# Regrouping the waits ahead of the last stores of a graph layer with a routed feed-forward part

## What is computed

```python
logits = xf @ router_w.T + router_b
idx = jnp.argmax(logits, axis=-1)
h = relu(einsum('nd,ndh->nh', xf, W1[idx]) + b1[idx])      # 256 -> 64
out = relu(einsum('nh,nhd->nd', h, W2[idx]) + b2[idx])     # 64 -> 256
x = x + out
```

## Time and profile before

| | us |
|---|---|
| median of 3 runs | 648.89 |
| lowest and highest | 646.72 and 649.28 |
| the profiled execution's own time | 648.73 |
| its span | 647.0 |
| POOL's last gather ends (in the span) | 591.7 |
| first of the 25 stores starts | 599.86 |
| last addition on DVE ends | 636.77 |
| last store starts | 640.76 |

### The profile page before, as it was taken

The page is one execution under the profiler, slowest core; times in us unless marked ns, Lnnn a source line. Parts: engine busy times, 40 slices in busy tenths (PEclk is TensorE's granted clock), DMA queues, the critical chain, the costliest instruction groups (busy, mean ns, idle before and its releaser), DMA issues.

```text
span 647.0 us, 10654 instructions
## 1 busy us (share of the span) xinstructions
PE 543.5 (84%) x3190; PEld 444.8 (69%) x3191; DVE 399.5 (62%) x1372; ACT 200.9 (31%) x406; POOL 443.4 (69%) x465
## 2 busy tenths in 40 slices
PE   0777998998888866899999999998999993289990
PEld 0676997866666665686878787886878762167880
DVE  6868776533343345455776767677566776716883
ACT  4666700000000010215552424242242452045540
POOL 6777777777777777777777777777777700374555
PEclk9969999999999987999999999999999996579996
DMA  8983333333333444334444544454444418464112
GB/s 274 256 251 103 105 101 98 106 98 106 102 106 103 114 155 131 106 98 145 134 140 136 146 133 146 125 151 131 122 150 124 146 46 241 110 198 137 66 66 71
DMA packets 41265, 85.37 MB, mean 132 GB/s; under 512 B 10665, under 2 KB 22890, under 8 KB 41011
## 3 DMA queue, kind: packets, MB, share of 16 engines
q0 software_dynamic: 21968, 61.03, 33.2%
q1 hardware_dynamic: 18372, 22.95, 11.2%
q10 hardware_dynamic: 864, 0.65, 0.3%
HBM read 71.79 MB, written 12.81 MB: 131 GB/s over the span
## 4 chain that ended last, share of the span: by engine, by line
PE 54%; POOL 17%; DMA 10%; DVE 8%; issue 8%; ACT 1%; ACTq 0%; POOLq 0%; DVEq 0%
PE ps L965 21%; POOL acc_raw L583 11%; PE ps L1027 11%; PE ps L1016 6%; DMA gath<-xn_d,src_i 4%; POOL gath L583 4%; PE ps L1233 3%; PE ps L1242 3%; DMA acc_raw<-xn_d,src_i 3%; PE ps L982 3%; DMA both<-rows_d,inv_i 2%; POOL both L669 1%; DVE raw_stats L1343 1%; DMA rel_of<-in_relation_of 1%; PE ps L1050 1%
## 5 line engine op out<-in xcount | busy, mean ns | idle before, releaser
L583 POOL DMA_INDIRECT gath<-xn_d,src_i x200 | 200.5, 1003 | 61.0 <-issue 52.4
L583 POOL DMA_INDIRECT acc_raw<-xn_d,src_i x168 | 164.0, 976 | 51.2 <-issue 43.6
L1400 DVE TENSOR_TENSOR wmat<-hit,wts 128x576 f32<-128x576 f32 x100 | 75.8, 758 | 137.2 <-PE ps L965 137.0
L965 PE MATMUL ps<-wmat,acc_raw 128*128 128x144 f32 x768 | 118.3, 300 | 31.4 <-DMA acc_raw<-xn_d,src_i 20.9
L965 PEld LDWEIGHTS ps<-wmat,acc_raw 128*128 128x128 f32 x768 | 105.7, 197 | 45.9 <-issue 29.0
L965 PE MATMUL ps<-wmat,gath 128*128 128x144 f32 x800 | 122.3, 294 | 6.8 <-DMA gath<-xn_d,src_i 6.6
L1424 DVE TENSOR_TENSOR acc_raw<-acc_raw,ps 128x144 f32 x392 | 100.6, 298 | 36.1 <-PE ps L965 35.1
L965 PEld LDWEIGHTS ps<-wmat,gath 128*128 128x128 f32 x800 | 107.9, 190 | 18.6 <-DMA gath<-xn_d,src_i 9.0
L669 POOL DMA_INDIRECT both<-rows_d,inv_i x25 | 24.1, 964 | 50.9 <-DVE inv_i L1690 42.6
L1027 PE MATMUL ps<-wk_et,acc_raw 128*128 128x256 f32 (+1 forms) x200 | 51.2, 380 | 0.0
L1027 PE MATMUL ps<-wq_wv,acc_raw 128*128 128x256 f32 (+1 forms) x200 | 51.0, 379 | 0.0
(11 more groups left out here) (225 smaller groups left out, 720.9 us busy)
## 6 DMA issues: line engine op xcount, KB each, us to landing
rows_d<-both SPq DMA_DIRECT2D x24, 256.0 KB, 2.2
gath<-xn_d,src_i POOLq DMA_INDIRECT x200, 2.7
both<-in_x SPq DMA_DIRECT2D x24, 128.0 KB
acc_raw<-xn_d,src_i POOLq DMA_INDIRECT x168, 2.8
both<-in_x SPq DMA_DIRECT2D x4, 640.0 KB, 10.6
xn_d<-both SPq DMA_DIRECT2D x4, 640.0 KB
acc_raw<-in_w_t SPq DMA_DIRECT2D x1, 2080.0 KB
acc_raw<-in_w_t SPq DMA_DIRECT2D x1, 2048.0 KB, 7.4
```

The source lines that it names most:

```text
L583: g.indirect_dma_start(place_of(n), None, table, bass.IndirectOffsetOnAxis(ap=src_i[:, n:n + 1], axis=0)).then_inc(done, 16)
L965: ins = t_.matmul(ps_edge[quarter][:, m * B * WIN:(m + 1) * B * WIN], place_of(n)[:, m * P:(m + 1) * P], wmat[:, k, :, :].rearrange("p b w ...
L1400: d.tensor_tensor(wmat[:, half * w:half * w + w, :, :], hit[:, :, :].unsqueeze(2).to_broadcast([P, w, B, WIN]), wts[:, :, cut].rearrange(" ...
```

## The change

The waits on `f_hid` are set at other stores: no longer ahead of each even store, but at the stores of a table, so that the stores go out by two, two, three, two, three, two, three, two, and the last six behind the last of the waits. The highest value, 14, is now awaited ahead of store 19 and not ahead of store 16. The reading of `lasts` moves ahead of that wait where both stand at the same store (now t = 0, 4 and 12; at t = 8, 16, 20 and 24 there is no wait on `f_hid`). The number of waits (9), readings (7) and stores (25) is the same.

```diff
-FIRST_STORES = 6
+OUT_AT = {0: 6, 2: 7, 4: 8, 7: 9, 9: 10, 12: 11, 14: 12, 17: 13, 19: 14}
...
             for t in range(NT):
                 n = moved(t)
-                if t % 2 == 0 and FIRST_STORES + t // 2 <= NG:
-                    pool.wait_ge(f_hid, FIRST_STORES + t // 2)
                 if t % FT == 0:
                     lasts = nc.values_load_multi_w_load_instructions(last_i[0:1, t:min(t + FT, NT)], engines=(pool.engine,), min_val=1, max_val=NPAIR)[1]
+                if t in OUT_AT:
+                    pool.wait_ge(f_hid, OUT_AT[t])
                 pool.wait_ge(f_y, lasts[t % FT])
                 pool.sem_inc(f_due, 1)
```

## The result

The changed kernel takes 644.37 us (median of 8 runs, 642.61 to 646.55) against 648.69 of the kernel before beside it (8 runs, 646.72 to 651.14). The ratio of the means is 0.9941 with a 95% interval of 0.9921 to 0.9962, so it is faster by 0.59% (0.38 to 0.79), which is 3.8 us (2.5 to 5.1). The forecast was 645.7.

The account below looks back on a forecast made before the run. POOL's queue of nine stores behind f_hid 14 was taken to bound the end; with six, DVE's last addition binds and store 24 starts 3.1 us earlier. Profiled 648.73 - 3.1 = 645.6, adjusted to the runs' median 645.7; range 643.8 to 647.6.

Parts of the forecast that it names:

- The bound of the kernel before: At the end, POOL's engine: nine stores left behind f_hid 14, following each other every 1.27 us without a break.
- The walk of the six stores: POOL's stores 19 to 24, each at the latest of engine, wait and sequencer; store 24 at 637.65, 3.1 us earlier.
- The cost that no row of before showed: On POOL, from an f_hid or pair wait to a store with idle engine and no reading: taken as 0.8 us.
- The reading ahead of store 20: On POOL's sequencer between stores 19 and 20: passes 2.1 us apart, 0.8 lost, taken back by later waits.
- Its terms for store 17: POOL's stores 14 to 16 through by 625.5, so store 17 starts near 625.5 and no backlog reaches store 19.
- the bounds of the walk: Wait-to-store step of 0.26 or 1.12 us in place of 0.8: gain 3.7 or 2.8, time 645.0 to 646.1.
- The reading ahead of the waits: At stores 0, 4 and 12: starts them some 1.4 us earlier, worth nothing at the end.
- The tail: POOL's drain behind the last store, ending 4.7 us after its engine time, was taken to follow the store.
- The drain of a fixed length: Rival at the program's end: POOL's drain lasts 9.0 us whatever the engine does, time stays 648.8; chance 0.10.
- The later reading: Rival at store 24: a reading of 1.4 us stands open behind the last additions, gain 1.7, 647.1; chance 0.09.
- Stores that hold up additions: Rival at DVE's adds meeting POOL's stores: half of 0.97 us per store costs 12 us, time 658; chance 0.05.
- the likelier branch of the forecast: No difference beyond 0.5% (3.24 us): 0.44 of the forecast's 0.76, 0.63 with the first two rivals.

Follow-up runs that it names:

- the grouping alone: The changed kernel, but the reading of the four numbers stays behind the wait on f_hid; 645.25 us against 647.89 of the kernel before, ratio 0.9956.
- the reading alone: The kernel before with its old places of the waits, but the reading ahead of the wait; 646.45 us against 647.89, ratio 0.9979.

## Why the prediction was right, and where it was off

**The bound of the kernel before** was read rightly: a queue of nine stores on POOL. With the reading ahead of the wait, nine, eight and six stores behind f_hid 14 give distances of 11.10, 9.82 and 9.37; the step from nine to eight is one store's 1.28, the step to six is cut off by the last addition.

**The walk of the six stores** holds, with store 20 earlier than forecast. Counted from the end of the last product (628.38 there, 627.98 here), stores 19 to 24 were forecast at 0.8, 2.9, 4.2, 5.5, 7.4 and 9.3; they start at 0.84, 2.68, 4.10, 5.38, 7.53 and 9.37. The cost that no row of before showed, a wait followed by an idle engine's store, was taken at 0.8 between 0.26 and 1.12; the runs show 0.81 to 0.85, and 0.88 for the last store with its address.

**The mis-sized terms** are small. The reading ahead of store 20 held it by less than the 2.1 of the earlier trace rows: store 20 starts 1.84 behind store 19. The load in that reading took 0.56 in the kernel before (the first row) and 0.33 here (the second):

```profile
L679 POOLq TENSOR_LOAD <-last_i x1: 556/556/556, 632.0 to 632.0; - x1
```

```profile
L677 POOLq TENSOR_LOAD <-last_i x1: 330/330/330, 628.6 to 628.6; - x1
```

Stores 20 and 23 were longer than those in a queue (1.11 and 1.15 in place of 0.97). None of this reaches store 24, which waits for addition 56. That addition ends 8.49 behind the last product and not 8.38 as before, and store 24 is late by as much. One register load on DVE's sequencer (line 498) took 0.49 us in the changed kernel in place of 0.34. In the grouping alone it took 0.49 too, and addition 56 ends at 8.49; in the three others in which VectorE does all the masking (the reading alone, the last wait ahead of store 17, no wait on f_hid) it took 0.34, and the addition ends at 8.34 to 8.38. Why the load is longer was not tried. This 0.1 is what lies between the gain of 3.0 in the trace and the forecast's 3.1.

Three sums of the prediction are a little off, without effect on its argument. Its terms for store 17 (0.8, 0.8 and three steps of 1.27 from 620.75) give 626.2 and not 625.5; the store did start 2.90 ahead of the last product's end, which is 625.5 in the kernel before, because the reading for store 16 cost nothing: that store starts 0.30 behind the one before it. The gain of 3.1 taken from the median gives 645.8 and not 645.7, and from the fastest run of before 643.6 and not 643.8. The measured 644.37 lies inside the range of 643.8 to 647.6, but under the 645.0 to 646.1 that the bounds of the walk gave.

**The reading ahead of the waits** was costed at nothing at the end, and the grouping alone shows that: 9.38 with it behind the wait, 9.37 with it ahead.

**The tail** was taken to follow the store, and did. That the profile's end of an indirect DMA on POOL is not its processor's end, as the Trainium skill has it (Perfetto Trace Analysis, the section on the DMA instruction of GPSIMD), agrees with a drain that always ends 4.74 behind it, but does not say how long that stretch is.

**The rivals.** The drain of a fixed length (0.10) fell with the 5.89 us. The later reading (0.09) did not come: the sequencer passes store 24 at 636.50, at the end of the last addition, and its reading was done by 635.8. Stores that hold up additions (0.05) fell with the kernel without waits: 422 ns on the mean, and over the whole part 422 for the 31 additions that overlap a store in time against 423 for the 25 that don't. The rule of the Trainium skill (SBUF — State Buffer, Who interferes with whom) that a DVE instruction with two SBUF inputs contends with a GpSimd instruction that reads SBUF shows no cost here.

**The chances.** The forecast put 0.63 on no difference beyond 0.5% and 0.32 on faster, since the mechanism ends at 3.1 us, 0.48%. The measured 0.59% lies beyond the line, with an interval that reaches across it. So the likelier branch of the forecast did not come by the measured figure, though its mechanism did. Grouping alone, whose end is the same to 0.01 us, gave 0.44% (0.26 to 0.62). The traces hold 3.0 us, which lies inside the interval of 2.5 to 5.1; whether the part of 3.8 beyond that is more than scatter stays open, and no run shows a mechanism for it.

## What to carry to other kernels

Where a wait lets a burst of equal steps go at the end of a program, count the steps behind the last wait: (steps - 1) times the spacing, against the last producer's end, tells at once how many may stand there and what the floor is. Two edits to the same queue don't add up; cost each with the other in place. When the floor is reached the next gain lies with the producer, not with the queue. And ask first whether the waits are needed: here the kernel without them ended as early as the one with the better table.

## What had not been expected of the hardware

POOL's drain ends 4.74 us behind its last indirect DMA however long the sequencer has been waiting in it (5.89 to 9.00 us), and the span 0.55 behind that. Some full stores on POOL took longer than the 0.97 us of a queue, and a pause ahead of them does not decide it: in the changed kernel 20 and 23 took 1.11 and 1.15 after one and 19 took 0.97; without waits store 21 took 0.97 after an idle 2.85, and store 18 took 1.17 after 0.30. What does decide it was not tried. And the waits on the first-layer products, which look like a shield for TensorE and VectorE, shielded nothing that could be seen: without them products stayed 3.82 us apart.
